# Another order of three TensorE products in every fourth step: the feed-forward norm's centre product ahead of the v projection, its variance product behind the scores, P's transposes last

## The reference, cut to what matters

```python
x = x + 0.5 * ffn_stack(layernorm(x))      # 6 layers, see below
x = x + mamba(layernorm(x))
x = x + 0.5 * ffn_stack(layernorm(x))

# one of the 6 layers of ffn_stack, with 16 heads of 64 and windows of 32 tokens
x = attn_layer(shift_tokens(x), ...) + x   # q, k l2-normalised and rotated, v;
                                           # scores against this window and the one before,
                                           # softmax, times v, times Wo
x = ffn_layer(shift_tokens(x), ...) + x

def ffn_layer(x, g, bln, W1, b1, W2, b2):
    mu = x.mean(-1, keepdims=True)
    var = ((x - mu) ** 2).mean(-1, keepdims=True)
    xn = (x - mu) / jnp.sqrt(var + 1e-05) * g + bln
    hg = xn @ W1 + b1
    a, gate = jnp.split(hg, 2, -1)
    return a * jax.nn.gelu(gate, approximate=False) @ W2 + b2
```

## Time and profile before

| | us |
|---|---|
| median of 3 runs | 3281.72 |
| lowest and highest | 3278.72, 3283.54 |
| the profiled execution, its span from first to last instruction | 3281.1 |
| PE busy in it | 3130.3 (95%) |
| DVE busy | 2721.8 (83%) |
| ACT busy | 2486.3 (76%) |
| POOL busy | 2434.9 (74%) |

### The profile page before, as it was taken

The page is one execution under the profiler, slowest core; times in us unless marked ns, Lnnn a source line. Parts: engine busy times, 40 slices in busy tenths (PEclk is TensorE's granted clock), DMA queues, the critical chain, the costliest instruction groups (busy, mean ns, idle before and its releaser), DMA issues.

```text
span 3281.1 us, 120591 instructions
## 1 busy us (share of the span) xinstructions
PE 3130.3 (95%) x51702; PEld 2520.7 (77%) x51702; DVE 2721.8 (83%) x3169; ACT 2486.3 (76%) x3160; POOL 2434.9 (74%) x1229
## 2 busy tenths in 40 slices
PE   7999999999999999998888999999999999999999
PEld 5888888888888887875333788888788888888787
DVE  7887888888888888877999888888888888888886
ACT  5777777787777777777676777778777778778776
POOL 6787787776776776762999778778768768778664
PEclk8999999999999999999999999999999999999999
DMA  3333233233233332231000323323323323323222
GB/s 121 89 80 87 71 93 86 68 91 86 72 88 85 75 84 66 71 75 42 20 0 1 98 67 80 91 72 85 92 72 81 94 71 81 97 66 90 69 67 66
DMA packets 142300, 245.23 MB, mean 75 GB/s; under 512 B 32397, under 2 KB 34638, under 8 KB 141774
## 3 DMA queue, kind: packets, MB, share of 16 engines
q1 hardware_dynamic: 141774, 237.51, 28.5%
HBM read 35.01 MB, written 1.05 MB: 11 GB/s over the span
## 4 chain that ended last, share of the span: by engine, by line
PE 84%; issue 5%; DVE 5%; POOL 3%; ACT 3%; DMA 0%; SPq 0%; ACTq 0%; DVEq 0%; POOLq 0%
PE PS L283 16%; PE PS L407 12%; PE PS L427 8%; PE PS L352 8%; PE PS L215 8%; PE PS L217 7%; PE PS L216 7%; PE PS L564 4%; PE PS L506 2%; PE PS L508 2%; PE PS L507 2%; PE PS L362 2%; PE PS L450 2%; POOL ARENA L1893 2%; DVE ARENA L1706 2%
## 5 line engine op out<-in xcount | busy, mean ns | idle before, releaser
L283 PE MATMUL PS<-C,ARENA 128*128 128x128 f32 x4608 | 619.7, 278 | 38.4 <-ACT ARENA L1025 11.4
L1777 POOL TENSOR_TENSOR ARENA<-ARENA 128x1024 f32<-128x1024 f32 x192 | 470.5, 2451 | 235.3 <-DVE ARENA L1359 234.5
L1785 POOL TENSOR_TENSOR ARENA<-ARENA,RN 128x1024 f32<-128x1024 f32 x192 | 365.3, 1903 | 367.7 <-ACT RN L960 367.7
L283 PEld LDWEIGHTS PS<-C,ARENA 128*128 128x128 f32 x4608 | 512.4, 141 | 119.1 <-issue 77.8
L1025 ACT ACTIVATE ARENA<-PS 64x1024 f32<-64x1024 f32 x384 | 390.5, 1017 | 182.2 <-PE PS L283 180.0
L215 PE MATMUL PS<-WL,XH 128*128 128x512 f32 x1152 | 500.0, 434 | 8.4 <-POOL XL L1744 4.0
L1771 POOL TENSOR_TENSOR ARENA<-ARENA 128x1024 f32<-128x1024 f32 x192 | 456.2, 2376 | 7.0 <-DVE ARENA L1341 7.0
L217 PE MATMUL PS<-WH,XH 128*128 128x512 f32 x1152 | 454.7, 395 | 0.1
L216 PE MATMUL PS<-WH,XL 128*128 128x512 f32 x1152 | 452.2, 393 | 0.0
L407 PE MATMUL PS<-ARENA 128*64 128x64 f32 x12288 | 403.0, 224 | 27.4 <-DVE ARENA L1399 14.0
L407 PEld LDWEIGHTS PS<-ARENA 128*64 128x64 f32 x12288 | 376.7, 138 | 60.8 <-issue 60.8
(11 more groups left out here) (163 smaller groups left out, 6419.1 us busy)
## 6 DMA issues: line engine op xcount, KB each, us to landing
ARENA<-ARENA SPq DMA_DIRECT2D x1152, 128.0 KB, 2.4
ARENA<-ARENA SPq DMA_DIRECT2D x768, 64.0 KB, 2.1
ARENA<-in_wqkv SPq DMA_DIRECT2D x36, 512.0 KB, 5.4
ARENA<-in_wo SPq DMA_DIRECT2D x12, 512.0 KB, 3.8
ARENA<-in_w SPq DMA_DIRECT2D x12, 341.0 KB, 3.1
ARENA<-in_w SPq DMA_DIRECT2D x12, 192.0 KB, 4.6
X<-in_xT SPq DMA_DIRECT2D x4, 256.0 KB, 4.6
out<-X SPq DMA_DIRECT2D x1, 768.0 KB, 3.3
```

The costliest lines, as they stand in the source:

```text
L283: last = nc.tensor.transpose(PS[:, slot, 128 * j:128 * j + 128], src[:, 128 * j:128 * j + 128], ident)
L1777: nc.gpsimd.tensor_tensor(KN[n % 2], KN[n % 2], T2, ALU.add).then_inc(k_add, 1)
```

## The change

In PE's loop the calls of a step get another order. In a step where all of them act, ffn_centre moves from behind the scores to between the q and the v projection; ffn_variance moves to directly behind the scores; p_transpose, which stood between the two, comes last. ffn_down moves only against calls that do nothing in its own steps. ACT's loop follows: ffn_square moves from behind split_input to between q_square and v_evacuate. No operation is added or removed, and no buffer changes.

```diff
                 q_project(s - 18)
+                ffn_centre(s - 23)
                 v_project(s - 20)
                 scores(s - 20)
+                ffn_variance(s - 23)
                 bias_products(s - 20)
                 carry(s - 19)
-                ffn_centre(s - 23)
                 ffn_down(s - 24)
                 p_transpose(s - 21)
-                ffn_variance(s - 23)
@@
                 q_square(s - 17)
+                ffn_square(s - 22)
                 v_evacuate(s - 19)
                 restore_tables(s - 23)
                 inverse_norms(s - 18)
                 carry_evacuate(s - 18)
                 split_input(s - 24)
-                ffn_square(s - 22)
                 ffn_rsqrt(s - 22)
                 p_evacuate(s - 20)
```

## The result

| | before | after |
|---|---|---|
| median, us | 3283.39 (20 runs) | 3287.94 (20 runs) |
| lowest to highest | 3277.15 to 3286.86 | 3280.92 to 3293.96 |
| the profiled execution's span | 3281.1 | 3285.9 |

The ratio is 1.0015, with a 95% interval of 1.0009 to 1.0021: about 5 us slower, a difference that only many runs show, and inside the band that the forecast called no change. The spans of the two profiles differ by 4.8 us, so they can be compared.

What follows compares the result with a forecast made beforehand. PE, busy for 95% of the span, was taken as the bound. The terms summed to +4.5 us on the profiled 3281.1, giving 3285.6, and 0.6 more for the median, said as 3286; range 3276 to 3294.

Steps and rivals of the forecast that it cites:

- A, the stall that goes: In centre steps, PE's q transposes no longer wait for ACT's copy of P: 44 x -0.46 = -20.2 us.
- B, the new wait: In centre steps, PE's variance product behind the scores waits 0.51 us for ACT's carry: 35 x 0.51 = +17.9 us.
- B's cover: In nine centre steps, breaks in PE's queue in or just behind the scores hide the wait for the carry: 4.6 us.
- The first rival: Breaks in the scores fall elsewhere, so the wait for the carry is paid 44 times: 4.6 us more, 3291; chance 0.15.
- C, the switches: PE's switches between kinds of matmul cost 2.84 instead of 2.78 us a centre step: 44 x 0.06 = +2.6 us.
- D, the copy of k: Centre product waits for ACT's copy of k in ten steps ahead of a new layer: 5 x 0.18 + 5 x 0.54 = +3.6 us.
- The second rival: The centre product waits for the copy of k in every centre step: 0.15 us each, 6.6 us, 3293; chance 0.15.
- E, the ends: Last centre step of each stack: centre product stands 1.2 us for the copy of k; +1.3 net, twice: +2.6 us.
- F, the last layer: Four last-layer centre steps: PE's wait for DVE swallows earlier delays and ends 0.39 us earlier: 4 x -0.50 = -2.0 us.
- The third rival: The variance product's wait for the carry vanishes, 3268, or vanishes in half of the steps, 3277; faster kernel; chance 0.15.

Runs made afterwards that it cites:

- the best version: Changed kernel with ACT's carry ahead of its copy of v, old order in each stack's last centre step, residual halving one step later: 0.9920, median 3256.0 us.

## Why the prediction was right, term by term

The sum said +4.5 us; the medians say +4.6. That agreement is luck. Two larger errors cancel, as shown below, and the breaks in the scores alone differ by 3.6 us between the profiles of the kernel before with and without an edit that doesn't touch PE. Term by term, against the profile after:

- **A, the stall that goes:** 0.46 in 44 steps. Right: 1.79 from output projection to q transposes everywhere, and the experiment with P's transposes ahead of the variance product brings 2.25 back.
- **B, the new wait:** 0.51 a step. Right: the start at 2.14 of the step, and 0.49 a step given back when the carry goes first.
- **B's cover:** nine steps, 4.6 us. The mechanism is right, the count isn't. A break ahead of the wait is hidden up to the wait's length (0.52 cost 0.03, 0.67 cost 0.26). But the long breaks of the nine steps weren't there any more: the centre steps' scores had 6.7 us of breaks before and 1.9 after, so the wait stands at L485 in 42 steps, not in 35, and hid about 1.7 us. The first rival had this right, that the breaks fall elsewhere. Its price didn't come, since there was less to hide: beyond 40 x 18.97 the up stretches had 7.1 us before, and beyond 40 x 18.02 they have 0.5 now. The prediction's remark that the rule quoted from the Trainium skill leaves no room for such breaks goes too far. That rule says that crossing into the next block of instructions is mostly hidden. The profile counts 416 packets in the larger of two instruction queues and 28 to 36 visible breaks at L352, so most crossings could well be hidden. No run tests what the breaks are.
- **C, the switches:** +0.06 a step. Wrong in sign. From L485 to L283 it is 0.93 now and from there to the second piece of k 1.11, together 2.04, where 0.96 + 1.17 = 2.13 had been added up. The 0.03 is the stand ahead of L485: in the run with the carry first, without the stand, it is 0.96. The 0.06 is what lies ahead of the transposes: behind L485 it is 1.11 whether PE had stood or not, and so it is behind the down product L564 in both kernels, while the 1.17 had been read where the transposes stand behind other instructions. The pair of stretches came out 0.02 shorter instead of 0.11 longer, 5 us over 40 steps.
- **D, the copy of k:** 0.18 and 0.54, five times each. The mechanism is right; the size was 0.2 in eight steps and 0.6 in two (0.39 and 0.40 printed at L450). In all other steps the centre product came just in time. The second rival is out.
- **E, the ends:** +2.6, measured +3.3. The wait is right, 1.16 where 1.2 was said, and the run with the old end agrees, within intervals that overlap. Not foreseen was the clock: it had been at half for the first pieces of the projection before and stays there for all of it now. So the close size is partly luck.
- **F, the last layer:** -2.0. This is the step that failed, with "Other consumers have room: the inverse norms reach POOL 0.94 later". The normalise did come earlier (1345.99 after against 1346.27 before, with the step itself 1.1 later), but I took the halving's 2.50 us as fixed. It grew to 3.65, the waits at L407 grew by 2.9 us in the four steps, and behind two of them PE went on at half clock for a while. The four steps lost 6 us instead of gaining 2. The room was checked for what waits on POOL, not for what runs beside it.

So the main part was forecast at about +3 and came out at -5 (5 us of that by the pair of stretches, most of the rest by fewer breaks), and the last layer at -2 and came out at +6: two errors of 8 us that cancel. The third rival, a smaller B, didn't happen, though making it happen is what the best version does.

## What to carry to other kernels

When a step is moved in an order written by hand, work out the new wait as carefully as the one that goes: here 0.46 us went and 0.51 came, because the product's slot was freed by an instruction behind the copy of v and the inverse norms in another engine's queue. Then look whether that instruction can go into idle time that the other engine already has; this was worth three times what the reordering cost. And check the irregular steps (last layer, ends) on their own: they are few, but they held the whole loss.

A moved step shifts whole chains against each other, so instructions that never depended on one another can meet. On DVE and POOL that changes their durations, and a duration read from the profile before is then no longer safe.

## What the runs showed of the hardware that was not expected

- A DVE instruction with two SBUF operands took 0.69 us alone and 2.30 beside a POOL instruction, whose own time went from 1.90 to 2.36. In the 24 cases of four runs (before, changed, and both with the late halving) in which DVE's half found POOL's instruction under way, it ended 0.54 or 0.55 us after POOL's. So a printed length can be mostly a wait for the other engine.
- The same operation with one operand from PSUM took 0.74 us with and without POOL beside it.
- A break in PE's stream ahead of a wait at a semaphore costs only what exceeds the wait: 0.52 us cost 0.03 and 0.67 cost 0.26 ahead of the wait for the carry, where without it 0.52 cost 0.57 and 0.71 cost 0.66 (the run with the centre product alone).
- The sum of these breaks goes from 12.1 to 19.2 us over the thirteen programs, and differs by 3.6 between two whose PE code is the same.
- After 2.24 us in which PE did nothing, the granted clock went to 0.50 in one step; after 2.42 us in the step before that it stayed at 1.00, and so it did after all four such waits in the run with the old end. What decides was not tried.
